# A queue's loop written out or turned by the engine: SyncE in the edge stage of a graph layer

## The reference

```python
h = concatenate([x[src], edge_attr], axis=1)            # 53125 x 192
h = relu(bn(h @ W1 + b1, g1, be1))                      # 53125 x 128, mean and variance over the edges
s = segment_sum(h, dst);  cnt = segment_sum(1, dst)     # per node
agg = where(cnt > 0, s / max(cnt, 1), 0)
h2 = relu(bn(concatenate([x, agg], axis=1) @ W2 + b2, g2, be2))
out = layernorm(x + relu(h2 @ Wl + bl))
```

## Time and profile before

| | |
|---|---|
| runs | 787.88 us median (785.38, 787.88, 788.54) |
| the profiled execution | span 785.2 us from its first to its last instruction, the fastest run 785.38 us |
| busy PE, DVE, ACT, POOL | 333.3, 353.6, 175.1, 435.1 us |
| instructions | 9030 |
| mean granted TensorE clock | 0.704 |
| edge stage | some 25 to 643 us |

### The profile page before, as it was taken

One profiled execution on the slowest core, in us unless ns is written; L12 is line 12 of the kernel. 1 busy time (PEld: TensorE's weight loads), 2 busy tenths in 40 slices (PEclk: granted clock), 3 DMA queues, 4 the chain that ended last, 5 costly groups with the idle time before them and its releaser, 6 DMA issues.

```text
span 785.2 us, 9030 instructions
## 1 busy us (share of the span) xinstructions
PE 333.3 (42%) x1695; PEld 268.2 (34%) x1695; DVE 353.6 (45%) x683; ACT 175.1 (22%) x453; POOL 435.1 (55%) x538
## 2 busy tenths in 40 slices
PE   4533341333422343240333321233140359999985
PEld 4422230222211232220222220221130229999955
DVE  4343162431624316253227153341341538777696
ACT  2111020110201102011002011110110145665565
POOL 4747657475674747747557757477475502333320
PEclk9767575666656656566556656666585668999998
DMA  7424243233332324332233332233241316777503
GB/s 221 108 78 122 81 123 97 73 113 94 107 97 82 104 90 126 84 114 76 71 97 101 105 92 71 67 105 106 74 121 40 97 55 167 235 214 227 169 1 82
DMA packets 64555, 84.19 MB, mean 107 GB/s; under 512 B 16777, under 2 KB 43192, under 8 KB 64535
## 3 DMA queue, kind: packets, MB, share of 16 engines
q1 hardware_dynamic: 39506, 39.10, 17.1%
q0 software_dynamic: 13312, 27.29, 14.0%
q10 hardware_dynamic: 11717, 17.61, 6.4%
HBM read 63.82 MB, written 20.08 MB: 107 GB/s over the span
## 4 chain that ended last, share of the span: by engine, by line
another core or an unknown queue 28%; issue 25%; PE 13%; DVE 13%; DMA 11%; SPq 4%; ACT 2%; POOL 2%; DVEq 1%; ACTq 1%; POOLq 0%
DMA res<-spill 4%; DVE psS L1093 4%; PE psH L784 3%; PE psC L784 3%; DMA work<-in_edge_attr 3%; DVE res L1086 2%; SPq L448 2%; DVE work L1086 2%; SPq L444 2%; PE psH L684 1%; DVE psX L1100 1%; PE psH L671 1%; DMA work<-ytab,srci 1%; DVE hotb L1075 1%
## 5 line engine op out<-in xcount | busy, mean ns | idle before, releaser
L602 POOL DMA_INDIRECT res<-ytab,srci x300 | 284.8, 949 | 106.9 <-issue 91.0
L722 PE MATMUL psC<-hotb,onesb 128*128 128x256 bf16 x104 | 26.0, 403 | 347.4 <-issue 324.7
L602 POOL DMA_INDIRECT work<-ytab,srci x104 | 99.0, 952 | 109.2 <-DVE psS L1093 59.3
L886 ACT ACTIVATE work<-res 128x512 f32 (+1 forms) x78 | 49.1, 629 | 387.2 <-DVE res L1086 183.1
L722 PEld LDWEIGHTS psC<-hotb,onesb 128*128 128x128 bf16 x104 | 11.1, 128 | 362.4 <-issue 335.5
L684 PE MATMUL psH<-w1e,work 128*128 128x256 f32 x200 | 80.2, 572 | 26.9 <-DMA work<-in_edge_attr 25.2
L1100 DVE TENSOR_TENSOR psX<-work,psX 128x512 f32<-128x512 f32 x104 | 72.1, 693 | 36.6 <-ACT work L886 20.9
L627 POOL TENSOR_TENSOR agg<-agg,srci 128x64 f32 x104 | 32.1, 309 | 87.1 <-ACT srci L968 86.3
L1166 DVE TENSOR_TENSOR work<-res,psX 128x512 f32<-128x512 f32 x103 | 70.1, 687 | 22.3 <-PE psC L784 9.6
L1086 DVE TENSOR_TENSOR res<-psH,res 128x512 f32 (+1 forms) x50 | 34.4, 688 | 98.1 <-remote 57.1
L1075 DVE TENSOR_TENSOR hotb<-iota,loc 128x256 bf16<-128x256 f32 x104 | 43.7, 421 | 76.2 <-remote 66.2
(11 more groups left out here) (170 smaller groups left out, 420.0 us busy)
## 6 DMA issues: line engine op xcount, KB each, us to landing
work<-in_edge_attr SPq DMA_DIRECT2D x104, 128.0 KB
hot_dram<-hotb ACTq DMA_DIRECT2D x26, 256.0 KB
spill<-work ACTq DMA_DIRECT2D x26, 256.0 KB
res<-spill SPq DMA_DIRECT2D x25, 256.0 KB, 3.4
res<-ytab,srci POOLq DMA_INDIRECT x300
hotb<-hot_dram SPq DMA_DIRECT2D x13, 256.0 KB, 3.0
work<-hot_dram SPq DMA_DIRECT2D x13, 256.0 KB, 3.6
h2x_dram<-agg ACTq DMA_DIRECT2D x12, 250.0 KB
```

What stands on the lines that cost most here:

```text
L602: pool.indirect_dma_start(rows[:, j * F:(j + 1) * F], None, ytab, bass.IndirectOffsetOnAxis(ap=srci[:, j, g:g + 1], axis=0)).then_inc(gath ...
L722: last = pe.matmul(psC[0][:, 0:U * WIN].rearrange("p (q w) -> p q w", q=U), onesb[:, :], hotb[:, :, j * WIN:(j + 1) * WIN], start=(j == 0) ...
L886: act.activation(sq[:, q % 2, :], slot(i, q), ACT.Square).then_inc(sq_ready, 1)
```

## The change

SyncE's steps 2 to 25 become an engine loop over i; step 1's loads and the first placing stay in front of it. In the loop the addresses and the values waited for are computed in registers. The columns are read with `nc.values_load`, without a check of their bounds. The counts no longer go to row g of `cnt` but to one of four rows (0, 32, 64, 96) by q, because the row must be known when the program is built. So groups g and g + 4 share a row, and a later window could overwrite an earlier one's counts where they overlap. VectorE therefore works out, beside the widest window, how far any group reaches over the start of the group four later, and the larger of the two (plus 64 for the second) is the `wide` by which the stage's form is chosen. It has a semaphore of its own, `s_wide`, for which every reader of `wide` waits. The sum over the rows of `cnt` takes all 128.

```diff
+QUAD = 32
...
+        lows = tail(NG)[0:1, :]
+        highs = tail(NG)[0:1, :]
...
             def place_counts(i):
 
-                bases = [sp.value_load(basei[0:1, U * i + q:U * i + q + 1], min_val=0, max_val=N) for q in range(U)]
+                bases = [nc.values_load(basei[0:1, bass.ds(U * i + q, 1)], engines=(mybir.EngineType.SP,),
+                                        min_val=0, max_val=N,
+                                        skip_runtime_bounds_check_because="dst holds node numbers") for q in range(U)]
                 sp.wait_ge(cnt_copied, i + 1)
                 for q in range(U):
-                    g = U * i + q
-                    sp.dma_start(cnt[g:g + 1, bass.ds(bases[q], WIN)], cnts[:, q * WIN:(q + 1) * WIN]
+                    r = QUAD * q
+                    sp.dma_start(cnt[r:r + 1, bass.ds(bases[q], WIN)], cnts[:, q * WIN:(q + 1) * WIN]
                                  ).then_inc(cnt_placed, 16)
 
             sp.wait_ge(s_idx, 1)
-            for i in range(1, NI):
+            for q in range(U):
+                load_ea(1, q)
+            place_counts(0)
+            with sp.Fori(2, NI) as i:
                 for q in range(U):
                     load_ea(i, q)
                 place_counts(i - 1)
...
+            sp.wait_ge(s_wide, 1)          # and before the same load on pool, pe, act, dve
             wide = sp.value_load(rowi[0:1, 0:1], min_val=0, max_val=N)
...
-                pe.matmul(psK[n % len(psK)][:, 0:cw], onesf[0:NG, :], cnt[0:NG, c0:c0 + cw], start=True, stop=True
+                pe.matmul(psK[n % len(psK)][:, 0:cw], onesf, cnt[:, c0:c0 + cw], start=True, stop=True
...
             link(dve.tensor_reduce(rowc[0:1, 0:1], psT[1][0:1, 0:NG], AX_X, ALU.max))
-            dve.tensor_copy(rowi[0:1, 0:1], rowc[0:1, 0:1])
+            dve.tensor_copy(lows, psT[0][0:1, 0:NG])
             link(dve.tensor_copy(basei[0:1, :], psT[0][0:1, 0:NG]))
+            link(dve.tensor_tensor(highs, psT[1][0:1, 0:NG], lows, ALU.add))
             dve.memset(col[:, C_M:C_M + 1], 0.0).then_inc(s_idx, 1)
+
+            link(dve.tensor_tensor(highs[:, 0:NG - U], highs[:, 0:NG - U], lows[:, U:NG], ALU.subtract))
+            link(dve.tensor_reduce(rowc[0:1, 1:2], highs[:, 0:NG - U], AX_X, ALU.max))
+            link(dve.tensor_scalar(rowc[0:1, 1:2], rowc[0:1, 1:2], float(WIN), rowc[0:1, 0:1], ALU.add, ALU.max))
+            dve.tensor_copy(rowi[0:1, 0:1], rowc[0:1, 1:2]).then_inc(s_wide, 1)
```

More of the change, by code:

```diff
@@ L92, in gnn_kernel @@
         mx = work[:, 0:4, :]
-        cnts = work[0:1, 1, 0:U * WIN]
         onesf = work[:, 3, F:2 * F]
         back = work[:, 4, :]
+        cnts = work[0:1, 1, 0:U * WIN]
         work2 = sb("work2", [P, 4, TILES * WIN])
@@ L216, in gnn_kernel @@
         s_idx = sem("indices_ready")
+        s_wide = sem("widest_window_ready")
         s_yps = sem("y_psum")
@@ L627, in add_window @@
                 pool.tensor_tensor(w, w, wsum[:, q, :], ALU.add).then_inc(agg_added, 1)
+            pool.wait_ge(s_wide, 1)
             wide = pool.value_load(rowi[0:1, 0:1], min_val=0, max_val=N)
@@ L771, in _ @@
             pe.matmul(psX[:, 0:F], onesf, work[:, 3, 0:F], start=True, stop=True).then_inc(s_ups, 1)
+            pe.wait_ge(s_wide, 1)
             wide = pe.value_load(rowi[0:1, 0:1], min_val=0, max_val=N)
@@ L950, in _ @@
             mark_edgeless(1)
+            act.wait_ge(s_wide, 1)
             wide = act.value_load(rowi[0:1, 0:1], min_val=0, max_val=N)
@@ L1170, in sum_step @@
                     maxes(i, q)
+            dve.wait_ge(s_wide, 1)
             wide = dve.value_load(rowi[0:1, 0:1], min_val=0, max_val=N)
```

## The result

The changed kernel takes 798.05 us (median of 4 runs, 795.88 to 802.29), the kernel before 786.74 in the same set (median of 4, one more than above): ratio 1.0142, 95% interval 1.0106 to 1.0179. It is slower by some 11 us. The number lies in the forecast's range, but the case that I called likeliest, no change, did not come; the "slower" rival in its small form (794 to 800) did.

A forecast was written before the change was run, and what follows sets the result against it. GpSimd's gathers set the edge stage's pace, with 95 us of pauses behind slowed SyncE instructions and TensorE counts. Only the second half's +2 us was priced: 785.2 to 787 profiled, 790 against the median; range 773 to 812 (8 in 10).

The forecast's parts named there:

- "slower" rival in its small form: SyncE's cycle ends last in the edge stage; drifts of 0.5 to 1 us a pair, 794 to 800; all slower forms 0.29.
- Step 1: SyncE's instructions in a step rise from 24 to 35, about 260 more in all.
- Step 2: SyncE's quick stretch: added load and loop instructions, less the checks saved, cost net some 0.5 us a step.
- Step 6: Four count rows instead of 104: same DMAs and TensorE time; price 0, bound +-0.3 us.
- Step 7: VectorE's start: +0.3 us ahead of `s_idx`, about 1 us behind it, covered by idle time; price 0.
- Steps 3 and 5: SyncE's slow-half loads go out later but fit; quick loads issue 1 us later, the last perhaps slow; price 0 each.
- if SyncE is not through its quick step: Slower rival's case: when the next slow stretch begins, 16 load instructions cost 19 us, not 3; all slower forms 0.29.
- Step 4: Second half of the edge stage: load 2's margin is 1 to 2 us; 0.5 us on some five pairs, +2 us.
- Step 8: Tail: SyncE's last columns, at most 8 instructions instead of twelve, plus loop exit; -1 to +1 us, taken 0.
- Fetches at the turn: Slower rival: each of SyncE's 24 loop turns waits 2 us for an instruction fetch; 790 to 802; chance 0.04.
- Written-out code is the cause: Faster rival: SyncE is slow because written out; 783 to 788, or as low as 700 if TensorE is freed; 0.26.
- Nothing happens: SyncE's loop repeats the same DMAs in the same order and pace; 784 to 794; chance 0.45 together with the forecast.

The follow-up runs named there:

- second trace: Another profiled execution of the unaltered changed kernel, from the third set, span 793.1 us; that set measured the kernel at 799.8 us, ratio 1.0178.
- idle increments: Semaphore increments nobody waits for, added to SyncE's steps written out without assertions or loop: 793.06 us with 30 instructions a step, 807.4 us with 46.
- half-written loop: Changed kernel with SyncE's loop over steps 2 to 21 and the last four steps written out: 794.91 us, ratio 1.0109.
- half-precision kernel: Kernel before with line 684's products taken from upper halves as bf16: 783.26 us, ratio 0.9961, on a slow chip; 681.15 us on the quick chip.

## Why the prediction was right in its range and wrong in its case

The limits of the stage were read rightly. On a slow chip SyncE and TensorE are slow while GpSimd gathers at 1.25 us, as the experiment with slower gathers bears out, and the forecast priced the change by it. What it missed is on which side of the quick window the loads come to lie. That the measured time lies in the range is owed to the slower rival's small form (0.5 to 1 us a pair, 794 to 800) and not to the case that I called likeliest.

*Step 1* said 35 instructions a step; there are 33, because only the second and the third load have an ALU_OP. SyncE's total rose by 203, not 260. *Step 2* held in its price: the quick loads take 2.06 us, and the turn 0.6 us against the 0.3 and the 0.2 for the first load that I gave. *Step 6* held as far as the runs can tell: written out again, with four rows, the ratio is 1.0019 (0.9979 to 1.0060). *Step 7* held: VectorE's first edge operation starts at the same time as in the earlier trace rows.

```profile
26.51 0.69 DVE L1102 COPY res<-psH 128x512 f32<-128x512 f32 x1 [4.25 <-issue]
```

*Steps 3 and 5* failed, by one error. I let the slow stretch begin behind the quick loads, at 204.6, and priced the quick loads at 0, with one at most falling into it. But the quick window closes at a time of its own: in before the first slow register instruction comes 5.7 to 8.4 us after GpSimd resumes, in 10 of its 12 pauses of over 4 us. The loads of before went out 4.4 us after GpSimd had resumed and were done at 6.4 (252.12 and 254.12, against 247.75). In the changed kernel they came to lie over this edge: only the first was still quick (208.18), or none was, and they began 10 us after GpSimd had resumed (258.36). That is 16 instructions at 1.3 us in place of 2 us, the very case that I named ("if SyncE is not through its quick step") and put at 29% with the milder forms. The pace was 1.3 us (26 instructions from 209.5 to 243.2), not 1.2. The four loads of the slow half then went out only at the clearing, the first at 243.89 in place of 228.14 and not 3 to 5 us later. Load 0 used up all that it had to spare, and the margins of 9 and 6 us of loads 1 and 2 shrank to some 2 and 3. I have not separated how much of the loss hangs on these loads and how much on the late quick ones. It did not cost the 2 or 7 us a pair that I gave to this rival. The clearing comes in every pause and lets SyncE catch up, and the pauses grew by 0.8 us a pair, 10.1 in all. *Step 4*, +2 us in the second half, is part of the same sum.

*Step 8* was right in one execution and wrong in the other. In the profiled one of the result the tail is +6.6 us, not -1 to +1. The eight column instructions that I counted are quick there; what counts is that the last loads fell on the slow side of the cycle (10.88 us). In the second trace they fell on the quick side (2.06 us), and the tail is that of before.

The rivals. *Fetches at the turn*: refuted for this body. The turn takes 0.63 us nearly each time on the quick chip, and the instruction queue moved 12 packets in the changed kernel where before moved 16. The rule of the Trainium skill (Runtime: NRT & Kernel Launch, section Instruction fetch mechanics), by which a taken branch out of what is held waits for a fetch, shows in none of these turns. That does not speak against the rule: whether a body of 33 instructions leaves what is held was not tested. *Written-out code is the cause*: refuted. The loop's instructions take 0.7 us as well, and on the quick chip hardly any does, written out or not. *Nothing happens*: true on the quick chip alone.

What stays open. The loop (1.0142 and 1.0178) costs more than idle increments do at 30 instructions a step (1.0078) and less than they do at 46 (1.0197). Three instructions lie between 30 and 33, which at 0.7 to 1.2 us each are 2 to 4 us, so the count may explain most of the loop's loss. Whether their kind or place adds to it no run shows. The half-written loop (1.0109) can't be told from either. TensorE's granted clock is a rival that I left out. Its mean fell from 0.704 to 0.658, and between the 30th us and the last gather TensorE was busy for 212 us in place of 183. The half-precision kernel ran at 0.615 and was no slower than before, so a low clock by itself does not slow this stage; what part it has in the 11 us is not shown.

Why one chip has no slow stretches is not known: the same program, the same pace of gathers, 105 us less. The Trainium skill (NOTIFIC — the notification-queue block, section 7.1 Overflow: three behaviours, one of which stalls the engine) describes that the path of an engine's trace records can hold the engine back, where its queue is set to stall and is not drained in time. A price for each recorded instruction (5.7 us for 4, 11.2 for 8) would suit it, and so do the DMA packets in the kept traces. In quick stretches the first packet of an edge load starts 1.0 to 1.4 us after the record of the instruction that issues it (medians of six traces). In slow ones it starts 1.8 us before that record (median in each of four traces; 226.35 and 228.14 in before). So the records there are some 3 us behind what SyncE does, about two instructions, and a load goes out earlier than its row says. No run here shows what makes them late, or whether the slow stretches occur when nothing is recorded.

No version here beats before on both kinds of chip. The slower gathers win 1.3% where the slow stretches are; where they are not, 16 x 1.50 a step stands against 16 x 1.25, some 100 us more by an estimate from these paces. It was not run there, nor were values between 1.25 and 1.50.

## What to carry to other kernels

A queue that runs at two speeds can have an edge. A step that just fits into the quick window has nothing to spare, and a little more (here 0.6 us at the turn, and placings that begin somewhat later) can put all of it on the slow side. So read when the window closes and not only what waits at its end. Where relief for either of two engines wins little, both may be late, and then an addition to either costs at once. A loop's price here is mostly its added instructions at the pace that the engine has at that place, so on a queue without slack count the register work (computed addresses, computed waits) and not only the branch. And take more than one trace before you put down a piece of a loss: the tail of one execution was not in the next.

## What the runs showed of the hardware

One program took 681.17 us on one chip and 786 to 792 on three others, 13 to 14% apart, with all runs of a set within 0.6% of its median; the traces of the kernels that ran on the quick chip have the same 1.249 us from gather to gather. On the slow chips, in stretches in which GpSimd gathers every 1.25 us, SyncE's instructions take 0.7 us and come 1.3 to 1.4 us apart, and TensorE's counts come 1.4 us apart for each of its recorded instructions. There SyncE's records also lag: an edge load's first packet starts 1.8 us before the record of its issue, and 1.0 to 1.4 us after it in quick stretches (medians). With a memset and a wait between the gathers, 1.50 us a gather, the slow stretches are gone on such a chip, and 0.25 us more at each of 400 gathers, 100 us, ends in a faster kernel.
